# Both half-head copies out of PSUM on VectorE instead of one on each of two engines

## The reference, cut to what matters

```python
# x: [4, 1024, 128]; 16 heads of 8 columns each; K = 21 bias terms a head
def attn(x, w_in, w_gate, b_gate, amplitudes, sharpness, offsets):
    k, v, q = split(x @ w_in, 3)                       # each [4, 16, 1024, 8] by heads
    scores = einsum('bhqd,bhkd->bhqk', q, k) / sqrt(8)
    scores = scores + tisa_bias(amplitudes, sharpness, offsets, 1024)[None]   # same for all batches
    attn = einsum('bhqk,bhkd->bhqd', softmax(scores), v)
    a, g = split(attn @ w_gate + b_gate, 2)
    return a * sigmoid(g)

x = x + attn(layernorm(x), ...)
x = x + fp8_quantised_linear(layernorm(x), weight, bias)
```

## Time and profile before

| | us |
|---|---|
| time, median of 3 runs (636.27 to 636.79) | 636.49 |
| the profiled execution, its own time | 637.52 |
| its span, first to last instruction | 635.7 |
| TensorE busy in the span | 583.5 (92%) |
| VectorE busy | 565.9 (89%) |
| ScalarE busy | 552.1 (87%) |
| GpSimd busy | 106.3 (17%) |

### The profile page before, as it was taken

The page is one execution under the profiler, slowest core; times in us unless marked ns, Lnnn a source line. Parts: engine busy times, 40 slices in busy tenths (PEclk is TensorE's granted clock), DMA queues, the critical chain, the costliest instruction groups (busy, mean ns, idle before and its releaser), DMA issues.

```text
span 635.7 us, 12652 instructions
## 1 busy us (share of the span) xinstructions
PE 583.5 (92%) x3979; PEld 160.7 (25%) x3979; DVE 565.9 (89%) x685; ACT 552.1 (87%) x610; POOL 106.3 (17%) x97
## 2 busy tenths in 40 slices
PE   5793498999999999999999999999999999999685
PEld 2452021222222222222222222222222222235442
DVE  5975497999999999999999999999999999955886
ACT  2863497999999999999999999999999999953663
POOL 5731510010101010101010101001010101105603
PEclk8797698999999999999999999999999999999855
DMA  9127542526161616151516253443525261400004
GB/s 231 55 56 188 151 105 43 121 43 128 35 140 24 143 23 141 29 133 39 129 45 121 57 105 65 97 88 75 110 54 120 49 124 38 128 18 7 1 1 132
DMA packets 29804, 53.88 MB, mean 85 GB/s; under 512 B 9318, under 2 KB 20971, under 8 KB 28651
## 3 DMA queue, kind: packets, MB, share of 16 engines
q1 hardware_dynamic: 29466, 53.35, 36.9%
q10 hardware_dynamic: 320, 0.33, 0.2%
HBM read 43.34 MB, written 9.16 MB: 83 GB/s over the span
## 4 chain that ended last, share of the span: by engine, by line
ACT 39%; issue 33%; PE 5%; DVE 4%; DMA 2%; POOL 2%; SPq 1%; ACTq 1%; DVEq 0%; POOLq 0%
ACT pbuf L985 16%; ACT split L985 16%; ACT pbuf L993 3%; PE ps L1175 3%; ACT split L993 2%; DMA qb<-m_scratch 2%; DVE kb L1418 1%; POOL kb L845 1%; PE ps L908 1%; DVE split L1413 1%; PE ps L1170 1%; ACTq L984 1%; ACT o_sbs L734 1%; DVE amax L1382 1%; DMA v_all<-last_rows 0%
## 5 line engine op out<-in xcount | busy, mean ns | idle before, releaser
L942 DVE TENSOR_TENSOR pbuf<-ps,t 128x1024 f32<-128x1024 f32 x192 | 230.0, 1217 | 22.7 <-PE ps L883 18.7
L942 DVE TENSOR_TENSOR split<-ps,t 128x1024 f32<-128x1024 f32 x192 | 231.4, 1222 | 12.4 <-PE ps L883 6.8
L985 ACT ACTIVATE pbuf<-pbuf 128x1024 f32<-128x1024 f32 x192 | 207.2, 1259 | 22.7 <-DVE pbuf L942 22.5
L883 PE MATMUL ps<-qb,kb 64*128 64x512 f16 x1024 | 184.1, 390 | 23.9 <-SPq L798 14.7
L985 ACT ACTIVATE split<-split 128x1024 f32<-128x1024 f32 x192 | 202.4, 1268 | 0.1
L908 PE MATMUL ps<-split,vst 128*32 128x512 f32 x1024 | 137.1, 609 | 1.0 <-ACT split L993 1.0
L908 PE MATMUL ps<-pbuf,vst 128*32 128x512 f32 x1024 | 136.4, 605 | 0.0
L883 PEld LDWEIGHTS ps<-qb,kb 64*128 64x128 f16 x1024 | 48.7, 93 | 311.5 <-DVE pbuf L942 115.9
L892 PE MATMUL ps<-t64s,ident 128*64 128x512 f16 x512 | 80.1, 393 | 0.0
L993 ACT ACTIVATE split<-ps 128x1024 f32<-128x1024 f32 x64 | 78.6, 1228 | 0.0
L993 ACT ACTIVATE pbuf<-ps 128x1024 f32<-128x1024 f32 x64 | 78.2, 1222 | 0.0
(11 more groups left out here) (140 smaller groups left out, 348.4 us busy)
## 6 DMA issues: line engine op xcount, KB each, us to landing
t<-g_scratch SPq DMA_DIRECT2D x16, 960.0 KB
kb<-k_scratch SPq DMA_DIRECT2D x120, 64.0 KB
t64s<-gh_scratch SPq DMA_DIRECT2D x16, 248.0 KB
t64s<-gl_scratch SPq DMA_DIRECT2D x16, 248.0 KB
qb<-q_scratch SPq DMA_DIRECT2D x60, 64.0 KB
x_sb<-in_L_attn_x SPq DMA_DIRECT2D x4, 512.0 KB, 6.6
q_scratch<-split SPq DMA_DIRECT2D x8, 256.0 KB, 3.3
k_scratch<-split SPq DMA_DIRECT2D x8, 256.0 KB, 3.5
```

The costliest lines, as they stand in the source:

```text
L883: last = eng.matmul(ps[:, u + c, :], kb[p][rows, keys], qb[p][rows, b * HALF:(b + 1) * HALF], start=True, stop=True)
L942: eng.tensor_tensor(slot(g, b), banks(unit(k), 2), t128[p][:, t * P:t * P + S], ALU.add).then_inc(z_ready, 1)
L985: eng.activation(buf, buf, ACT.Exp).then_inc(p_ready, 1)
```

## The change

`copy_half` copies both halves with `tensor_copy`. The `c` = 1 copy leaves ScalarE's stream inside the loop, with its waits, and enters VectorE's in the same group 1, behind the bias addition of tile 1. The `c` = 0 copy stays where it is, behind that of tile 0. Behind the loop, ScalarE still copies the last head's `c` = 1 half. The 15 copies of `c` = 1 inside the loop move (seven of `p` = 1, eight of `p` = 0).

```diff
         def copy_half(eng, p, c):
 
             src, dst = ps[:, 6 + c, :], o_sb[p][:, S - 1 - c * HALF:(S - 1 - (c + 1) * HALF if c == 0 else None):-1]
-            if c == 0:
-                return eng.tensor_copy(dst, src)
-            return eng.activation(dst, src, ACT.Copy)
+            return eng.tensor_copy(dst, src)
...
                                 eng.wait_ge(o_stored[0], i * (16 * B) + 16 * B)
                                 copy_half(eng, 0, 0).then_inc(o_ready[0], 1)
+                            if b == 1 and g == LAG - 1:
+
+                                with eng.If(i > 0):
+                                    eng.wait_ge(groups_done, i * (2 * GPH) + SETS)
+                                    copy_half(eng, 1, 1).then_inc(o_ready[1], 1)
+                            if b == 1 and g == GPH + LAG - 1:
+                                eng.wait_ge(groups_done, i * (2 * GPH) + (GPH + SETS))
+                                copy_half(eng, 0, 1).then_inc(o_ready[1], 1)
...
-                            if b == 0 and g == LAG - 1:
-
-                                with eng.If(i > 0):
-                                    eng.wait_ge(groups_done, i * (2 * GPH) + SETS)
-                                    eng.wait_ge(o_stored[1], i * (16 * B))
-                                    copy_half(eng, 1, 1).then_inc(o_ready[1], 1)
-                            if b == 0 and g == GPH + LAG - 1:
-                                eng.wait_ge(groups_done, i * (2 * GPH) + (GPH + SETS))
-                                eng.wait_ge(o_stored[0], i * (16 * B) + 16 * B)
-                                copy_half(eng, 0, 1).then_inc(o_ready[1], 1)
                 eng.wait_ge(groups_done, H * GPH + SETS)
                 eng.wait_ge(o_stored[1], NH2 * 16 * B)
-                copy_half(eng, 1, 1).then_inc(o_ready[1], 1)
+                eng.activation(o_sb[1][:, HALF - 1::-1], ps[:, 7, :], ACT.Copy).then_inc(o_ready[1], 1)
```

## The result

| | before | after |
|---|---|---|
| time, median (lowest to highest), 14 runs each | 636.64 us (634.78 to 640.57) | 639.15 us (637.72 to 644.92) |
| ratio of the two | | 1.0044, 95% interval 1.0024 to 1.0063 |
| profiled execution | 637.52 us, span 635.7 | 641.59 us, span 639.8 |
| first copy of a head's half to the last | 109.82 to 565.49: 455.67 us | 111.62 to 569.73: 458.11 us |
| from one head's copy to the next | 30.49 us | 30.63 us |

The changed kernel is slower by 0.44%, some 2.8 us by that ratio and 2.5 by the medians. The spans differ by more, 4.1 us, and the table shows why they must not be read whole: 1.8 us of it lie ahead of the first copy, where nothing was changed, and 2.44 in the loop.

The account below looks back on a forecast made before the run. TensorE and ScalarE both pace at 3.75 us a group, with a 0.49 stall a head from ScalarE's copy. Fifteen heads 0.17 longer (2.5) plus the first head's extra 0.25 give +2.8: 636.49 + 2.8 = 639.3 us, range 637.7 to 643.5.

Parts of the forecast that it names:

- What the change takes away: Group 1 of each head: ScalarE loses 0.48 us of work, TensorE's 0.49 stall would go, −7.3 us over 15 heads.
- VectorE's price of 0.60: Behind tile 1's addition in group 1: the second copy delays VectorE's next addition by 0.60 to 0.61 us.
- The first new stall, 0.20: TensorE's scores of tile 1 of group 2 wait for tile 2's late addition, 0.20 us a head.
- The second, 0.46: TensorE's scores of tile 3 of group 2 wait for ScalarE's late exponential of tile 3, 0.46 us a head.
- The head, 0.17 longer: Each head: the old stall of 0.49 becomes 0.20 + 0.46 = 0.66 us, 15 × 0.17 = 2.5 us.
- The soft term: Tile 2 of group 1: the exponential behind the wait taken as 1.06 us; at 1.32 the sum nears +6.7.
- Rival 1: The late exponential in group 1 keeps its full length; TensorE loses 0.43 us a head, 643.2 us; chance 0.15.
- ScalarE idles 0.9 us: In front of tile 2 of group 1, ScalarE waits about 0.9 us for VectorE's addition.
- The first head, 0.42: The first head starts from another state, with a stall of 0.26; it grows by 0.42 us, 0.25 more than 0.17.
- Rival 2: VectorE's second copy in group 1 finds cover: 634.4 us partly, 629.2 entirely; chance 0.10.
- Rival 3: Stalls of 0.49 and 0.66 a head nearly cancel, no measurable difference: 636.5 to 637.7 us; chance 0.10.
- Costed at nothing: the DMAs: Denominators' DMA, issued once both copies are done, leaves about 0.2 us earlier; its chain has a whole head; no cost.

Follow-up runs that it names:

- e1: The kernel before with ScalarE's 15 copies inside the loop replaced by a bare signal, that half not computed: 629.22 us, ratio 0.990.
- e2: The changed kernel plus a spare ScalarE copy of 512 columns from SBUF where its old copy stood: 640.17 us, ratio 1.0067.
- e3: The changed kernel with VectorE's second copy cut to 256 columns, the rest of that half not computed: 633.76 us in one run.
- e4: The changed kernel with VectorE's second copy one place later, behind tile 2's addition in group 1: 639.11 us, ratio 1.0031.

## Why the prediction was right, step by step

- *What the change takes away.* ScalarE's 0.48 us caused the stall of 0.49: e1 leaves 0.04 of it. Right in the mechanism; the 7.3 us for the loop was a little high, since the first head's stall is only 0.26 and 0.04 stays in each: e1's loop is 6.5 us shorter.
- *VectorE's price of 0.60.* It is 0.60 behind each of the 30 copies in the loop, and 1.13 to 1.14 lie ahead of each. Right.
- *The first new stall, 0.20.* Measured 0.19. *The second, 0.46.* Measured 0.44. *The head, 0.17 longer.* Measured 30.634 − 30.489 = 0.145, in the mean of the distances. The 0.02 to 0.03 between is the sum of what both stalls were taken too long.
- *The soft term.* The exponential behind the wait lasts 1.06 (the row at 329.63), not 1.32. Rival 1, which hung on it, would have meant 30.9 a head. It falls.
- *ScalarE idles 0.9 us.* This step was mis-sized. The exponentials of tiles 1 and 2 start at 328.03 and 329.63, 1.60 apart where 0.95 is the pace: 0.65 idle. I had carried over ScalarE's starts of the kernel before, which run ahead of VectorE's: tile 3 of group 0 starts at 322.87, 0.12 ahead of VectorE's copy, and now at 326.18, 0.12 behind it. The end of tile 2's exponential hangs on the addition alone, so nothing followed from it, and e2 shows that there is room for 0.52.
- *The first head, 0.42.* The first distance went from 30.23 to 30.63, so 0.40.
- *The sum, +2.8.* The loop is 2.44 us longer. The medians say 2.5. The forecast of 639.3 lies 0.15 from the 639.15 measured, closer than the runs' scatter of several us allows to claim, and partly by luck: the rise was put 0.3 too high, on a median of the kernel before (636.49, from 3 runs) that came out 0.15 higher over 14.
- *Rival 2,* the second copy with cover: the break-even lateness that I gave for tile 2's addition, 0.44, fits e3, where 0.33 brings the head to 30.37, 0.12 under that of the kernel before, in the heads without the odd 0.10.
- *Rival 3,* no difference to be measured: it drew its line at 0.2%. The interval of the ratio begins at 0.24%, just clear of it; what excludes it is the distance between heads, longer by 0.14 to 0.15 in every head from the second on.
- *Costed at nothing: the DMAs.* For the change this held in its effect: VectorE never waits for the denominators, no head but the first waits for a load, and the granted clock reads 1.00 from 109.5 to 569 us. But the denominators don't always leave 0.2 earlier: counted from VectorE's first copy they leave at 2.51 in eight of 15 heads, against 2.69 before, and at 2.85 to 3.10 in six, where SyncE is still issuing the stores of the head before. And "the chain behind it has a whole head for itself" was too generous as a reason. The next head's loads, which hang on the same issue, have 0.5 to 2.2 us to spare in the kernel before and down to 0.3 in the changed one, and e4, with a copy 1.1 us later in a shorter head, used that up.

## What to carry to other kernels

When two engines run at the same pace and a third is near it, price a moved instruction at the place where it stands, not by its engine's busy share: walk the few instructions from it to the next wait of the pacing engine, in starts and not in durations. Relief on one engine only counts up to the lateness of the other; here 0.45 us a head was to be had; the copy's first place (behind tile 1) cost 0.60 and so gave back more than that, its second (behind tile 2) left a gain of 0.2. And before shifting anything on a DMA queue, ask for every transfer behind it which instruction of an in-order engine waits for it, and what stands behind that.

## What the runs showed of the hardware that was not expected

- The listed length of an activation grows in a row without gaps. The same copy lasts 0.59 us in the first head of the kernel before and 0.86 from the sixth on (L734 has 587 ns at least, 861 in the median), while in each of the 15 heads it ends 0.49 behind the exponential in front of it and the next one starts 0.48 behind its start. A wait sets the length of an exponential back: 1.06 and 1.01 in the changed kernel. So what grows reads as time spent behind the instruction in front, and says nothing on the price. The line of L734 in the kernel before:

```profile
L734 ACT ACTIVATE o_sbs<-ps x16: 587/861/865, 111.6 to 566.4; 128x512 f32<-128x512 f32 x16
```

- Much of what sets one trace apart from another lies outside the loop's steady part. In the kernel before TensorE waits 2.26 us for the second head's loads at about 100 us, in the changed kernel's trace 3.08, and in both it then runs at a granted clock of 0.5, the 1.2 GHz level, for some us; in the changed kernel's trace the products' x8 row takes 1.93 there, 1.06 elsewhere. From one kernel's trace to another's the first copy starts between 106.8 and 111.6 us. That the scatter among the runs of one kernel comes from there too is likely but not shown, since each kernel has one trace.

```profile
103.57 0.61 PE L881 MATMUL ps<-qb,kb 64*128 64x512 f16 x2 [3.08 <-DMA qb<-m_scratch]
104.11 1.93 PE L906 MATMUL ps<-split,vst 128*32 128x512 f32 x8
```
